# The first expert layer: every expert for every token, or token tiles sorted by expert

## The reference

```python
gate = xn @ wg_W + wg_b + (genre_embed @ gg_W + gg_b)     # xn: x after an RMS norm
gate_w = softmax(gate); topk_w, topk_i = top_k(gate_w, 2)
h1 = relu(einsum('bsh,ehm->bsem', x, W1) + b1)            # H 128, M 256, E 8
h2 = relu(einsum('bsem,emn->bsen', h1, W2) + b2)
out_e = einsum('bsen,enh->bseh', h2, W3) + b3
c = einsum('bseh,bse->bsh', out_e, cw)                    # cw: topk_w at the two chosen experts, else 0
```

## Time and profile before

| | |
|---|---|
| Time, median of 3 runs | 546.63 us (543.91 to 548.27) |
| Span of the profiled execution | 541.2 us |
| PE, DVE, ACT, POOL busy | 91%, 58%, 51%, 25% |
| First expert layer with what it carries, first product to `scores` of step 0 | 10.9 to 136.4 us |
| From there to the end | 404.8 us |

### The profile page before, as it was taken

The page is one execution under the profiler, slowest core; times in us unless marked ns, Lnnn a source line. Parts: engine busy times, 40 slices in busy tenths (PEclk is TensorE's granted clock), DMA queues, the critical chain, the costliest instruction groups (busy, mean ns, idle before and its releaser), DMA issues.

```text
span 541.2 us, 7612 instructions
## 1 busy us (share of the span) xinstructions
PE 494.7 (91%) x2782; PEld 345.1 (64%) x2782; DVE 315.8 (58%) x826; ACT 278.7 (51%) x414; POOL 136.3 (25%) x136
## 2 busy tenths in 40 slices
PE   5899799998989999999999988999999999889980
PEld 4578678886545555554897865445555554669970
DVE  4654444567778787764263577877788663402223
ACT  6734344552546566667454653556656555205640
POOL 5755622331711101200000000101111005231551
PEclk9999899999999999999999998999999999899995
DMA  8970200000700000020000000000000002540003
GB/s 323 303 234 2 78 1 0 1 1 1 307 5 0 1 2 0 1 79 0 2 1 0 1 2 1 1 0 1 0 1 2 0 1 94 249 107 4 19 18 120
DMA packets 12868, 26.57 MB, mean 49 GB/s; under 512 B 1293, under 2 KB 10120, under 8 KB 11808
## 3 DMA queue, kind: packets, MB, share of 16 engines
q1 hardware_dynamic: 11392, 22.91, 12.5%
q0 software_dynamic: 1440, 3.18, 1.9%
HBM read 22.11 MB, written 5.26 MB: 51 GB/s over the span
## 4 chain that ended last, share of the span: by engine, by line
PE 77%; DVE 10%; ACT 5%; issue 3%; DMA 3%; POOL 2%; POOLq 0%; DVEq 0%; SPq 0%; ACTq 0%
PE PS L436 13%; PE PS L468 11%; PE PS L453 10%; PE PS L690 5%; PE PS L579 5%; PE PS L613 5%; PE PS L581 5%; PE PS L580 5%; PE PS L730 3%; PE PS L721 3%; DVE mx L1153 3%; PE PS L342 3%; PE PS L421 2%; PE PS L422 1%; PE PS L443 1%
## 5 line engine op out<-in xcount | busy, mean ns | idle before, releaser
L1153 DVE TENSOR_REDUCE mx<-PS 128x1 f32<-128x512 f32 x256 | 164.6, 685 | 41.8 <-PE PS L436 39.3
L854 ACT ACTIVATE wc_late<-PS 128x1024 f32<-128x1024 f32 x128 | 123.9, 1022 | 62.2 <-PE PS L453 62.0
L436 PE MATMUL PS<-Kp,Qs 128*128 128x512 f32 x256 | 95.9, 438 | 6.9 <-DVE mx L1153 5.2
L436 PEld LDWEIGHTS PS<-Kp,Qs 128*128 128x128 f32 x256 | 44.7, 190 | 70.4 <-DVE mx L1153 40.3
L453 PE MATMUL PS<-Qm,Kp 128*128 128x512 f32 x256 | 75.2, 415 | 0.8 <-DVE Qm L1165 0.6
L468 PE MATMUL PS<-wc_late,v_c 128*16 128x512 f32 x512 | 67.3, 598 | 0.7 <-ACT wc_late L854 0.7
L1438 POOL CAST Kp<-Ks 32x512 fp32r<-32x512 f32 x40 | 24.3, 607 | 135.0 <-ACT Ks L833 133.1
L453 PEld LDWEIGHTS PS<-Qm,Kp 128*128 128x128 f32 x256 | 46.5, 190 | 18.1 <-ACT wc_late L854 3.8
L579 PE MATMUL PS<-wc_late_r 128*128 128x512 f32 x96 | 41.7, 435 | 1.1 <-POOL xT_yT_r L1400 0.6
L1052 DVE TENSOR_SCALAR work<-PS,early 128x512 f32<-128x512 f32 x32 | 22.6, 747 | 25.1 <-PE PS L581 25.1
L954 ACT ACTIVATE work<-PS,late 128x160 f32<-128x160 f32 x64 | 19.8, 396 | 32.5 <-PE PS L721 32.5
(11 more groups left out here) (244 smaller groups left out, 743.5 us busy)
## 6 DMA issues: line engine op xcount, KB each, us to landing
wa<-wa_dram SPq DMA_DIRECT2D x8, 512.0 KB, 9.0
wa<-wc_dram SPq DMA_DIRECT2D x2, 2048.0 KB, 9.8
wc_late<-wc_dram SPq DMA_DIRECT2D x2, 2048.0 KB, 11.1
wb<-wb_dram SPq DMA_DIRECT2D x1, 2048.0 KB, 15.6
sel<-sel_dram POOLq DMA_DIRECT2D x2, 1024.0 KB, 5.6
late<-late_dram SPq DMA_DIRECT2D x1, 1572.0 KB, 14.9
packed_rows<-ao SPq DMA_DIRECT2D x1, 1290.0 KB, 22.9
wb<-packed_rows SPq DMA_DIRECT2D x5, 258.0 KB, 4.3
```

What stands on the lines that cost most here:

```text
L436: filled(mm(p, Qs[:, G % 3, qt * P:(qt + 1) * P], Kp[:, G % 3, j, :], start=True, stop=True), (L, "max", G, qt, j))
L854: A(E4[:, 2 * (i % 2) + jp, :, :], p, ACT.Exp, scale=float(HD[L]) ** -0.5).then_inc(taken[f"s{jp}"], 1)
L1153: V.reduce_max(mx[:, G % 2, qt, j:j + 1], p, AX.X).then_inc(taken[filled_at[key][0]], 1)
```

## The change

The first expert layer is computed for chosen pairs only.

- Token tile 0 (128 tokens) stays dense: eight items n = 0 to 7, one for each expert, with plain fp32 matmuls of 128 columns (2 for h1, 4 for h2, 2 for the output) from `wa`. Their results wait in `y_dense`.
- The other seven tiles form two groups `GA`: tiles 1 to 3 (group 0) and 4 to 7 (group 1). Every token is in it twice, once for each of its two experts. DVE and PE count ranks within experts (`experts_a`, `count_a`, `places_a`), and each expert's tokens take whole tiles of 128 places. A group so has at most 2 x tiles + 7 padded tiles: 13 and 15, always all computed. `expert_of` holds the expert of each padded tile.
- POOL puts the rows of x by indirect transfers into DRAM (`x_put_d`, cleared before), two for each token tile; SP reads them back (`rows_in`), PE turns them (`xp`). Items 8 to 20 and 21 to 35 are the padded tiles, eight matmuls each.
- The weights of each of those 28 items are loaded anew from DRAM, 526 KB, into a ring of four (`wa_ring`, 1028 numbers in a row with the biases). SP reads the expert's number into a register (`value_load`) and issues the transfer; a slot is free when `a3` of the item four before it is full.
- Results go by SP to DRAM (`y_put_d`), and POOL fetches each token's two rows back by indirect transfers; `sum_a(g)` on DVE weights and adds them to `c0`. `sum_a(1)` lies in step 3 of the attention's main loop, `cT` of batch 1 moves from step 2 to step 4.
- No splitting into high and low parts in this layer. Evacuations are on 128 x 128 pieces, h1 by ACT, h2 by ACT in the dense items and DVE in the others, outputs by ACT.
- The two clears for the third layer and `wb` move behind the first ring loads. The carried attention work moves to items 29 to 36.

The core of the diff:

```diff
+GA = ((1, 4), (4, 8))
+NTA = tuple(2 * (b - a) + EA - 1 for a, b in GA)
+NDA = EA
+NIA = NDA + sum(NTA)
+RING = 4
...
-            out = ({2: [("cT", 1)], 6: [("qk", 1, 0)], 9: [("v", 1)]},
+            out = ({3: [("sum_a", 1)], 4: [("cT", 1)], 6: [("qk", 1, 0)], 9: [("v", 1)]},
...
+        a_jobs = {(3, 2): [("count_a", 0)], (6, 2): [("count_a", 1), ("gates_a",)],
+                  (7, 0): [("xp", 0, 0)], (8, 0): [("xp", 0, 1)], (9, 0): [("xp", 0, 2)], (10, 0): [("xp", 0, 3)],
+                  (9, 2): [("weightsT_a", 0)], (10, 2): [("bias_a", 0)], (11, 2): [("weightsT_a", 1)],
+                  (12, 2): [("bias_a", 1)], (13, 1): [("field", 0)], (14, 1): [("field", 1)],
+                  (14, 0): [("xp", 1, 0)], (18, 0): [("xp", 1, 1)], (20, 0): [("xp", 1, 2)], (22, 0): [("xp", 1, 3)],
...
+                  (29, 1): [("sum_a", 0)], (29, 2): [("cT", 0)], (30, 1): [("qk", 0, 0)], (30, 2): [("v", 0)],
+                  (31, 1): [("stackK", 0), ("stackK2", 0)], (31, 2): [("stackQ", 0)],
+                  **{(32 + k // 2, 1 + k % 2): [half] for k, half in enumerate(halves)}}
...
             def a_h1(n):
+                g, i = item_a(n)
+                if g is None:
+                    pe.wait_ge(wa_in[n], 16)
+                    x = xT[:, 0:P]
                 else:
+                    pe.wait_ge(ring_in[(n - S0) % RING], 16 * ((n - S0) // RING + 1))
+                    wait_taken(pe, ("xp", g, i // 4))
+                    x = xpT[:, i * P:(i + 1) * P]
+                p, w = claim(("a1", n), ("p2", "p3")[n % 2]), weights_of(n)
                 for c in range(2):
+                    last = mm(p[:, c * P:(c + 1) * P], w[:, c * P:(c + 1) * P], x, start=True, stop=True)
                 filled(last, ("a1", n))
...
             a_h1(0)
+            for n in range(NIA + 1):
+                for k in a_jobs.get((n, 0), []):
+                    a_job(*k)
+                if n + 1 < NIA:
+                    a_h1(n + 1)
+                if n:
+                    a_out(n - 1)
+                for k in a_jobs.get((n, 1), []):
+                    a_job(*k)
+                if n < NIA:
+                    a_h2(n)
+                for k in a_jobs.get((n, 2), []):
+                    a_job(*k)
...
+            def ring(s):
+                g, i = item_a(S0 + s)
+                sp.wait_ge(expert_of_set, g + 1)
+                if s >= RING:
+                    wait_full(sp, ("a3", S0 + s - RING))
+                e = sp.value_load(expert_of[0:1, g, i:i + 1], min_val=0, max_val=EA - 1)
+                sp.dma_start(wa_ring[:, s % RING, :], wa_d[:, bass.ds(e, 1), :].rearrange("p a n -> p (a n)")
+                             ).then_inc(ring_in[s % RING], 16)
...
+            def results(g):
+                for i in range(NTA[g]):
+                    n = (S0, S1)[g] + i
+                    if n - S0 + RING < sum(NTA):
+                        ring(n - S0 + RING)
+                    wait_taken(sp, ("a3", n))
+                    sp.dma_start(y_put_d[g][i * P:(i + 1) * P, :], y_a[:, (n - S0) % RING, :]
+                                 ).then_inc(y_out[(n - S0) % RING], 16)
+
+            for s in range(RING):
+                ring(s)
+            rows_in(0)
             sp.wait_ge(zero_ready, 3)
             blank = ao[:, :, :].rearrange("p t d -> p (t d)")
             sp.dma_start(packed_d.rearrange("(t p) c -> p t c", p=P),
                          blank[:, 0:ROW].unsqueeze(1).to_broadcast([P, NST, ROW])).then_inc(zeroed, 16)
             sp.dma_start(pair_d.rearrange("(r p) d -> p r d", p=P),
                          blank[:, 2 * D:3 * D].unsqueeze(1).to_broadcast([P, NPAIR // P, D])).then_inc(zeroed, 16)
+            rows_in(1)
+            results(0)
             sp.dma_start(wb[:, :, :], wb_d).then_inc(wb_in, 16)
+            results(1)
...
+                pool.wait_ge(x_clear[g], 16)
+                pool.wait_ge(put_a_ready, g + 1)
+                for t in range(*GA[g]):
+                    for k in range(2):
+                        pool.indirect_dma_start(out=x_put_d[g],
+                                                out_offset=bass.IndirectOffsetOnAxis(ap=put_a[:, k, t:t + 1], axis=0),
+                                                in_=x_tok[:, t, :], in_offset=None, bounds_check=NTA[g] * P - 1,
+                                                oob_is_err=False).then_inc(x_put[g], 16)
```

More of the change, by code:

```diff
@@ L137, in build @@
         E4 = wc_late[:, 0:4, :].rearrange("p a (b c) -> p a b c", b=2)
[L140 to L146, removed]
+        spare, wb_r = f32r_at["wc_late"], f32r_at["wb"]
         wb_high = [spare[:, 6144 + e * MB:6144 + (e + 1) * MB] for e in range(EB)]
@@ L634, in first_of @@
                         at.append(("m1" if free % 2 else "m0", "pv"))
-                    (second if L else first)["job"](name, *at)
+                    second["job"](name, *at)
             pe.wait_ge(gate_w_ready, 1)
@@ new lines, in a_h2, with a_out @@
+            def a_h2(n):
+                p, w = wait_full(act, ("a2", n)), weights_of(n)
+                if n >= 2:
+                    wait_full(act, ("a3", n - 2))
+                for c in range(2):
+                    o = 4 * MA + 2 + c
+                    last = A(h2_a[:, n % 2, c, :], p[:, c * P:(c + 1) * P], ACT.Relu, bias=w[:, o:o + 1])
+                last.then_inc(taken[filled_at["a2", n][0]], 1)
+            def a_out(n):
+                p = wait_full(act, ("a3", n))[:, 0:P]
+                if n < NDA:
+                    A(y_dense[:, n, :], p, ACT.Copy).then_inc(taken["m0"], 1)
+                else:
+                    s = n - S0
+                    if s >= RING:
+                        act.wait_ge(y_out[s % RING], 16 * (s // RING))
+                    A(y_a[:, s % RING, :], p, ACT.Copy).then_inc(taken["m0"], 1)
@@ new lines, in place_keys @@
+            def place_keys(L, groups):
+                for G in groups:
+                    wait_taken(pool, (L, "stack", G, 0))
+                    for j in range(HPG):
+                        rows = slice(SL * j, SL * (j + 1))
+                        nc.gpsimd.tensor_copy(Kp[rows, G % 3, j, :], Ks[rows, G % 2, :]).then_inc(Kp_set, 1)
+                        pool.wait_ge(Kp_set, HPG * (L * KEYS + G - 3) + j + 1)
+            for g in range(2):
+                pool.wait_ge(y_got[g], 16 * 2 * (GA[g][1] - GA[g][0]))
@@ L1511 @@
         "wg_b": rep(a["L0_cond_wg_b"]), "gg_b": rep(a["L0_cond_gg_b"]),
-        "b1a": cols(a["L0_cond_b1"]), "b2a": cols(a["L0_cond_b2"]), "b3a": rows(a["L0_cond_b3"]),
+        "steps": rep(P * np.arange(TPB, dtype=f4)), "lower": rep(P * np.tril(np.ones((EA, EA), f4), -1)),
+        "tile_at": rep(P * np.arange(EC, dtype=f4)), "before": np.triu(np.ones((P, P), f4), 1),
+        "b3a": rows(a["L0_cond_b3"]),
         "cond": rows(cond.T), "iota": rep(np.arange(EC, dtype=f4)), "ident": np.eye(P, dtype=f4),
```

430 lines of the change are left out of this document (258 added, 172 removed).

## The result

The kernel after takes 574.2 us (median of 4 runs, 573.5 to 578.0), the kernel before in the same comparison 546.2 us (543.9 to 548.3): ratio 1.052, 95% interval 1.048 to 1.057. It is slower by 28 us where 536 us were forecast, outside the range. The profiled execution has a span of 571.6 us against 541.2.

A forecast was written before the change was run, and what follows sets the result against it. PE was taken as the bound before, waits after: `scores` starts at 125.5 us instead of 136.4, 10.9 earlier, with 404.8 behind it, span 530.3; plus 5.4 between span and median, 535.7, taken as 536. Range 513 to 557.

The forecast's parts named there:

- the first part: Expert stage before the change: PE is the bound; 6.0 us of PE an item, 96 us for 16 items.
- step 1: Start until item 8: DMA queue, count, routing, puts and rows let item 8 start at about 33.3 us.
- step 3: Ring pace: item 16 at 58 us, items 16 to 28 at 2.5 us each, `wb` + 5, to 95.5.
- rival (a): Refills hidden, items 12 to 28 at 1.5 us, clears not in the way: 513 us; chance 0.18.
- Step 2: Item 8 to item 12: the fifth ring load stands behind clears and `rows_in(1)`; item 12 starts at 50 us.
- Step 4: Items 29 to 36 with the attention's beginning: 30 us, `scores` at 125.5 us, 10.9 us earlier than before.
- Step 5: Behind `scores`: fetch of group 1 and `sum_a(1)` costed at nothing, up to 5 us if the fetch is late.
- (c): Slow clock: PE stays at its slow level in ring items and step 4, 10 us more, 546 us; chance 0.16.
- (b): Slower refill chain through the register: cycle 7.5 us, 3.75 an item, 557 us; decides from 6.3; chance 0.16.
- the two gaps: Sign: PE idle near 23 to 33 us and 40 to 50 us.
- `scores` at 125: Sign: `scores` of step 0 first starts at 125 us, against 136.4 before.
- the 405 us behind it: Sign: the stretch behind the start of `scores` stays at 405 us, as the same program.

The follow-up runs named there:

- e2: Kernel after, with the 28 sorted items using resident weights (expert n mod 8), no refills or register loads: 548.8 us, ratio 1.006.
- e9: e6 with `rows_in(0)` issued ahead of the first four ring loads: 572.7 us, ratio 1.052.
- e10: Kernel after with ring of 12, clears and `wb` behind the last result, early count, rows of group 0 before the ring loads: 548.7 us, ratio 1.008.
- e12: e10 with 50 unread bf16 matmuls in a stand of PE, `sum_a(1)` split over steps 3 and 4, `cT(1)` at step 5: 543.0 us, ratio 0.995.
- e3: Kernel after with the load of `wb` issued behind the last result instead of between the two groups: 569.2 us, ratio 1.046.
- e4: Kernel after with 64 instead of 128 moving columns in every expert matmul from item 2 on: 595.4 us, one run.
- e6: Kernel after with PE's count of group 0 at iteration 1 and of group 1 at iteration 3: 574.4 us, ratio 1.051.
- e11: Kernel after with a constant expert (s mod 8) in place of the register load in the ring loads: 570.7 us, ratio 1.046.
- e1: Kernel after with a weight ring of 12 slots, fifth to tenth refill issued before the two clears: 566.2 us, ratio 1.040.
- e5: e1 with the two clears and `wb` issued behind the last result: 559.2 us, ratio 1.023.
- e8: Kernel after with `sum_a(1)` left out and `cT(1)` back at step 2: 570.9 us, ratio 1.044.

## Why the prediction was wrong

**The step that failed** is "so 0.117 us each", in the first part, and with it "what is left of PE: 36 items x 8 matmuls x 0.117 = 34 us". The row counts 16 records, and I took a record for a matmul. It is 36 x 1.87 = 67 us. What PE could give back was 29 us and not 62, and an item's floor, which I had at 1.5, is 2.3 us (e2); my own sum for it, with 0.45 and 0.9 for the two PE terms, gives 2.1. The counts of the earlier trace rows beside the code would have shown it: 256 records of L613 for 16 items of 8 matmuls (4 token tiles, 2 halves each; the 16 in the description of the kernel before is the number of records). Of the 41.3 us it makes, by my estimate, 5.7 in step 1 (22.2 for 16.5) and 2.9 in step 3 (0.44 us for each two of 13 items). It weighs more in the floor: e2 takes 46.6 us from item 12 to item 29 with no refill, where I had 45.5 with all of them and rival (a) 25.5, so that (a) at 513 could not happen in this order.

**Step 1** (+8.3). The dense items pace the count: at 2.3 us each `count_a(0)`'s result is read at 22.2, not at 16.5, and the sixth put starts at 31.7, not at 25.3, the puts going at 1.28 us as forecast. Behind it I had 2.2 us until the rows are issued, from the earlier trace rows; it was 5.0, and 4.0 to 5.5 in the nine profiles with ring loads ahead, against 2.2 without them (e2). The ring loads are not all of it, since with them behind the rows it was 3.0 to 4.2 (e9, e10, e12).

**Step 2** (+3.7). The wait was where I put it, but not for the clears alone: SP was through the second clear at 43.3 and then stood for the turn of group 0 on PE, 8.9 us, since `rows_in(1)` reuses its buffer.

**Step 3** (+5.2 and +9.1). Both disputed terms were right: the register load 0.8 forecast, 0.71 measured; the landing 3.55 forecast, 3.6 the median of the seven landings that the trace of the kernel after has (3.6 to 3.8 in e3, e4, e6 to e9 and e11). By the Trainium skill (Runtime: NRT & Kernel Launch, Instruction fetch mechanics) a register load takes about 200 ns; the load's own record is 0.27 us here, but the 0.71 that SP loses contain the arithmetic and the check around it. The 3.2 us for the landing that the prediction has from the Trainium skill (DMA: Bandwidth & Descriptors, Anatomy of one DMA) comes from that section's fit for transfers issued by GpSimd; these are SP's, and the measured 3.6 decides. With h1 and the output at 0.45 us each the cycle is 0.07 + 0.71 + 3.6 + 0.45 + 0.45 + 0.17 = 5.45, where I had 5.03. From one ring load of SP to the second behind it are 5.6 to 5.8 us at best, and 6.9 to 7.5 from 77.38 to 94.56, where turns of group 1 and `field` go along. That is what I left out of 13 x 2.5: items 16 to 24 took 26.4 us where I had 20, and with no wait for a refill they still take 22.9 to 24.4 (e1, e2, e5, e12). `wb` cost 5.7 where I had 5, and e3 gives it back. Items 12 to 15 (+5.2) started cold and had field and bias work between them, at 3.3 us each.

**Step 4** (+6.9): e2 has 36.1 us there with all weights at hand, so that the refills are no part of it. 3.2 of it is a mistake in counting: item 29's first product stands in iteration 28, so nine iterations lie behind it, and I added up eight. Of the others those with `qk` and `v` (4.7 where I had 3) and the last three (13.9 where I had 12.1) are longer; how much of that is the doubled PE time is not shown.

**Step 5** (+8.1), costed at nothing. I asked whether the fetch would be late and not what `sum_a(1)` does to DVE: 3.74 us in one piece on an engine that sets PE's pace there, nor at which clock the loop starts. Leaving the sum out takes 4.3 us from its two steps (e8), splitting it 3.5, and the clock 2.7 from the first two (e12); e12 gives back 7.0 of e10's 8.5 in all.

**The rivals.** The outcome is none of them alone. (c), the clock, is shown by windows and by e12; (b)'s mechanism is there, the cycle being 5.6 to 7.5, though with the register load and the landing at my values and not at its. It was said to decide from 6.3 us; with the true floor the change had no gain to lose, and every wait counted against it from the start. Of the signs, the two gaps came (29 to 40 and 55 to 62 us), as did PE's waits for `wc_late<-wa_dram` and 22 MB more of transfers; `scores` at 125 and the 405 us behind it did not. One thing stays open: the stands in which SP and the other engines are held together.

## What to carry to other kernels

Count the records of a matmul group against the loop that makes them before dividing a duration by them; fp32 ones come twice. Before costing the waits of a change, work out its floor with every wait removed, and if that is no better than now, hiding the transfers alone will not save it: here the resident-weight run gave 548.8 against 545, and e12 came to 0.995 of the kernel before only with the routing, the clock and the sum mended as well. And where a layer with little work stands ahead of a dense loop, its bill has a tail, in the clock and in each lump of work that it hands to the engine that paces the loop.

## What the runs showed of the hardware

- Engines can stand together, with "remote" as the releaser, while four ring loads are issued: DVE for 6.4 to 6.6 us where 1.8 to 2.0 is its plain wait. The four issues took SP 4.75 to 6.56 us where they did (after, e5 to e8) and 2.59 to 4.54 where not (e1, e3, e4, e11). SP is held too: a bounds check whose record is 0.02 us elsewhere takes 0.60 and 0.51 in the kernel after (27.24 and 28.81 us). That instructions are fetched late behind the transfers is a guess that the trace doesn't bear out: from 27.3 to 33.7 us no packet of an instruction queue moves.
- Reading a number from SBUF into a register and making a transfer's address from it holds SP for 0.71 us (e11), 0.27 of it the record of the load.
- An fp32 matmul takes PE the same time with 64 columns as with 128: 1.06 us for four at 2.4 GHz, 1.91 at 1.2 (e4 beside the kernel after).
- PE stayed at 1.2 GHz for 120 us with 64-column fp32 matmuls that filled up to 98% of the time (e4, one execution).
- Issuing eight loads of 526 KB took SP 8.88 us in e10 and 13.49 in e5, although both have the clears behind the whole layer. In e10 each issue takes 0.33 us and they start 1.15 to 1.60 apart, so that most of the 8.88 is the register work, eight times. In e5 the first four start 2.2, 3.6 and 2.3 apart, with register instructions of up to 0.71 us, and ACT is held beside them: a second stand.
